# Routing of tokens to experts in four groups of tiles, with place masks made during attention and the weights gathered beside the rows

## The reference, cut to what matters

```python
x = x + attn(layernorm(x), ...)          # state space mixer, 64 heads
x = x + xattn(layernorm(x), ctx, ctx)    # 32 query heads, 8 key heads
x = x + ffn(layernorm(x), ...)

def ffn(x, router_logits, gating_einsum, linear, per_expert_scale, router_scale):
    router_input = x * rsqrt(mean(x * x) + 1e-6) * rsqrt(512) * router_scale
    logits = router_input @ router_logits                     # 8 experts
    probs = softmax(logits)
    choices = top_2(logits)
    weights = probs / sum(probs of the two chosen)
    # each token goes to its two experts: tokens are sorted by expert
    gate_out = rows @ w_gate[expert]                          # 512 -> 2 x 512
    activation = gelu(gate_out[0]) * gate_out[1]
    out = (activation @ linear[expert]) * per_expert_scale[expert]
    return sum over the two choices of weights * out
```

## Time and profile before

| | us |
|---|---|
| median of three runs | 1507.66 (1503.03 to 1511.12) |
| profiled execution | 1507.27 |
| its span | 1505.4 |
| mean granted TensorE clock | 0.937 of full |
| TensorE busy | 1345.9 |
| VectorE busy | 861.5 |
| ScalarE busy | 723.1 |
| GpSimd busy | 569.1 |

### The profile page before, as it was taken

How to read it: one execution, slowest core, us unless ns; L and a number is a source line. 1 busy time by engine, 2 the same in 40 slices (tenths; PEclk the granted TensorE clock), 3 DMA queues, 4 the chain that set the end, 5 groups by cost and what they waited for, 6 DMA issues and landing times.

```text
span 1505.4 us, 22777 instructions
## 1 busy us (share of the span) xinstructions
PE 1345.9 (89%) x7700; PEld 747.6 (50%) x7700; DVE 861.5 (57%) x1727; ACT 723.1 (48%) x1387; POOL 569.1 (38%) x852
## 2 busy tenths in 40 slices
PE   5699999999999999988788887854999999999997
PEld 4466566666666665653333333334444444444443
DVE  4887888879797978677888888335011111111111
ACT  2577666677676666672777766630111111111110
POOL 2355565645555547672233322123022222222221
PEclk9899999999999999997989889765999999999999
DMA  9000000000000000001000000012233444344322
GB/s 325 11 8 5 8 5 6 7 3 11 1 12 1 12 1 9 14 2 59 37 19 19 20 19 15 27 63 101 105 84 98 129 137 119 56 133 126 56 42 29
DMA packets 38017, 72.76 MB, mean 48 GB/s; under 512 B 16272, under 2 KB 20624, under 8 KB 36880
## 3 DMA queue, kind: packets, MB, share of 16 engines
q1 hardware_dynamic: 27968, 48.03, 9.0%
q0 software_dynamic: 8736, 20.45, 7.4%
q10 hardware_dynamic: 1200, 2.82, 0.5%
HBM read 148.75 MB, written 19.92 MB: 112 GB/s over the span
## 4 chain that ended last, share of the span: by engine, by line
PE 65%; DVE 18%; issue 5%; DMA 4%; POOL 4%; ACT 3%; SPq 0%; POOLq 0%; ACTq 0%; DVEq 0%
PE work_ps L502 11%; PE gate_ps L1377 9%; PE up_ps L1377 9%; PE down_ps L1365 9%; PE work_ps L574 6%; DVE conv L783 6%; PE work_ps L507 3%; PE work_ps L596 3%; PE work_ps L999 2%; DVE maxes L1148 2%; PE mturn_ps L507 2%; PE decay_ps L990 2%; DVE mix L699 2%; PE decay_ps L584 2%; DMA x_sb<-x_dram 1%
## 5 line engine op out<-in xcount | busy, mean ns | idle before, releaser
L502 PE MATMUL work_ps<-xnT,w_in 128*128 128x256 f32 (+1 forms) x1216 | 302.3, 394 | 1.6 <-DVE xdt L823 0.9
L699 POOL TENSOR_TENSOR mix<-decay,cbm 128x512 f32<-128x512 f32 x128 | 182.5, 1428 | 213.0 <-ACT decay L694 177.2
L502 PEld LDWEIGHTS work_ps<-xnT,w_in 128*128 128x128 f32 (+1 forms) x1216 | 220.8, 190 | 64.6 <-issue 33.3
L690 ACT ACTIVATE decay<-decay_ps 128x512 f32<-128x512 f32 x256 | 154.2, 603 | 110.2 <-PE decay_ps L584 108.8
L1148 DVE TENSOR_REDUCE maxes<-work_ps 128x2 f32<-128x512 f32 x256 | 166.7, 684 | 46.5 <-PE work_ps L975 45.5
L1507 POOL DMA_INDIRECT out_dram<-y_out,ids x39 | 61.8, 1586 | 337.4 <-DVE y_out L1476 270.4
L783 DVE SCALAR_TENSOR_TENSOR conv<-raw,conv_w,conv 128x256 f32<-128x256 f32 x240 | 179.7, 753 | 6.9 <-ACT conv L650 1.1
L1062 ACT ACTIVATE prob<-decay_ps 128x512 f32<-128x512 f32 x256 | 143.2, 607 | 81.3 <-PE decay_ps L990 80.1
L1483 DVE TENSOR_TENSOR act<-gelu,up_ps 128x512 f32<-128x512 f32 x39 | 26.8, 688 | 269.7 <-PE up_ps L1377 269.7
L694 ACT ACTIVATE decay<-decay 128x512 f32<-128x512 f32 x256 | 164.0, 641 | 4.7 <-PE work_ps L502 3.0
L1377 PE MATMUL gate_ps<-w_e,xgT 128*128 x312 | 143.1, 602 | 2.2 <-ACT xgT L1396 1.7
(11 more groups left out here) (253 smaller groups left out, 1893.6 us busy)
## 6 DMA issues: line engine op xcount, KB each, us to landing
w_e<-c_experts_dram SPq DMA_DIRECT2D x39, 3072.0 KB
normed_tokens<-r_xn SPq DMA_DIRECT2D x17, 256.0 KB, 2.2
out_dram<-x_sb SPq DMA_DIRECT2D x17, 256.0 KB, 3.0
x_sb<-x_dram SPq DMA_DIRECT2D x1, 3584.0 KB, 22.4
w_in<-c_w_inT_dram ACTq DMA_DIRECT2D x1, 2560.0 KB, 12.0
w_in<-c_w_inT_dram SPq DMA_DIRECT2D x1, 2048.0 KB, 8.5
w_out<-c_w_outT_dram SPq DMA_DIRECT2D x1, 2048.0 KB, 13.5
RT<-cum_scratch SPq DMA_DIRECT2D x32, 48.0 KB
```

Of the source, the lines that this page charges most:

```text
L502: m = e.matmul(ps[0:width, at:at + L], w_in[:, k, col:col + width], xnT[b % 2][:, k, :], start=(k == 0), stop=(k == KD - 1))
L690: e.activation(decay[s % 5][:, :], decay_ps[s % 3][:, :], ACT.Relu, scale=-1.0).then_inc(piece_done[stage], 1)
L699: return e.tensor_tensor(four(mix[s % 5]), four(decay[s % 5]), cb, ALU.mult)
```

## The change

The routing has four groups: tiles 0 to 7, 8 to 11, 12 to 13 and 14 to 15. The counting is done for each group by its own two matmuls ("c_count", TensorE, in one of the five shared banks), and "c_slots" (VectorE) adds the counts to those of the tiles before and gives the place of each token. So the place masks can be made by group: all 32 are made on GpSimd ("place"), 16 in batch 5 of the attention, 8 in batch 7, the rest behind it. The masks hold token numbers (less 2048) instead of ones and are f16; the second operand of the place matmuls is a plain mask of tiles, f16 with 39 columns. Unfilled slots get a number of their own.

For the last two tiles, VectorE adds the attention output of tile 14 and GpSimd that of tile 15 ("attend_v", "attend"). Their logits are made from centred rows ("last_center": the mean is taken off, no scale), and the scale of both norms is worked out beside it on VectorE ("last_newton") and applied to the logits. The router pieces of batch 6 stand four slots later (`late`).

The weights of the tokens are written as 8 more columns of normed_tokens ("c_weight_out"), whose rows grow from 512 to 520 numbers, and are gathered with the rows; in each expert tile VectorE picks the tile's column by two small operations (`row_weight`). The owners are worked out behind the token numbers. The copies of x_sb to the output are issued after each batch ("out_in"). Three memsets, a copy and an addition move into "r_init". Cut to its core:

```diff
-ROUTED = [(3, 0, 8), (6, 8, 14), (7, 14, 16)]
+ROUTED = [(3, 0, 8), (5, 8, 12), (6, 12, 14), (7, 14, 16)]
+ROUND = 1.5 * 2.0 ** 23 * P
...
+        if b == NB - 1:
+            continue
+        late = 4 if b == NB - 2 else 0
         put(f + 12, ("r_stats", b), ("r_newton", b))
         for t in range(TPB):
-            put(f + 16 + 2 * t, ("r_xn", b, t), ("r_store", b, t))
-            put(f + 17 + 2 * t, ("r_turn", b, t))
-            put(f + 18 + 2 * t, ("r_copy", b, t))
-            put(f + 19 + 2 * t, ("r_logit", b, t))
-            put(f + 20 + 2 * t, ("r_keep", b, t))
-    for g, (last, _, _) in enumerate(ROUTED):
-        f = n * (last + 1)
-        put(f + 20, ("c_scale", g), ("c_newton", g))
-        put(f + 26, ("c_logit", g), ("c_exp", g))
-        put(f + 28, ("c_rank", g))
-        put(f + 30, ("c_weight", g))
+            put(f + 16 + late + 2 * t, ("r_xn", b, t), ("r_store", b, t))
+            put(f + 20 + late, ("out_in", b, t))
+            put(f + 17 + late + 2 * t, ("r_turn", b, t))
+            put(f + 18 + late + 2 * t, ("r_copy", b, t))
+            put(f + 19 + late + 2 * t, ("r_logit", b, t))
+            put(f + 20 + late + 2 * t, ("r_keep", b, t))
...
+    for g, at in enumerate((4 * n + 20, 7 * n, 7 * n + 27)):
+        put(at, ("c_scale", g), ("c_newton", g))
+        put(at + 3, ("c_rank", g), ("c_count", g))
+        put(at + 5, ("c_logit", g), ("c_exp", g))
+        put(at + 6, ("c_slots", g))
+        if g < 2:
+            put(at + 9, ("c_weight", g), ("c_weight_out", g))
+    for t in range(12):
+        for c in range(2):
+            put(n * 5 + 4 * t if t < 8 else n * 7 + 8 + 4 * (t - 8) + 2 * c, ("place", c, t))
+    f = n * NB + 9
+    put(f, ("attend_v", NB - 1))
+    for t in range(TPB):
+        put(f, ("last_stats", t), ("last_center", t))
+    put(f, ("last_newton",), ("c_weight", 2), ("c_weight_out", 2), *[("place", c, t) for t in (12, 13) for c in range(2)])
+    for stage in ("r_turn", "r_copy", "r_logit"):
+        put(f, *[(stage, NB - 1, t) for t in range(TPB)])
+    for t in range(TPB):
+        put(f, ("r_xn", NB - 1, t), ("r_store", NB - 1, t), ("out_in", NB - 1, t), ("r_keep", NB - 1, t))
+    put(f, ("c_rank", 3), ("c_count", 3), ("c_logit", 3), ("c_exp", 3), ("c_slots", 3), *[("place", c, t) for t in (14, 15) for c in range(2)])
+    put(f, ("c_base",), ("c_spread", 0), ("c_weight", 3), ("c_weight_out", 3), ("c_spread", 1))
...
-    tokens = nc.dram_tensor("normed_tokens", [(NT + 1) * P, DIM], F32).ap()
+    tokens = nc.dram_tensor("normed_tokens", [(NT + 1) * P, DIM + NE], F32).ap()
...
+            elif stage == "c_count":
+                g, = key
+                _, first, end = ROUTED[g]
+                both = sel[2][:, first:end, :].rearrange("p t e -> p (t e)")
+                width = (end - first) * NE
+                e.wait_ge(*done("r_init"))
+                e.wait_ge(*done("c_rank", g))
+                e.matmul(work(*piece)[:, 0:width], m_ones[:, :], both, start=True, stop=True)
+                e.matmul(work(*piece)[:, NT * NE:NT * NE + width], earlier[:, :], both, start=True, stop=True).then_inc(piece_done[stage], 1)
...
+            elif stage == "last_center":
+                t, = key
+                e.wait_ge(*done("last_stats", t))
...
+                e.activation(a_xn[t][:, :], x_sb[:, (NB - 1) * TPB + t, :], ACT.Identity, bias=neg_mean[:, t:t + 1]).then_inc(piece_done[stage], 1)
...
+            elif stage == "attend_v":
+                b, = key
+                e.wait_ge(*done("pv_out", b, 3))
+                e.tensor_tensor(x_sb[:, b * TPB, :], x_sb[:, b * TPB, :], o_tok[b % 2][:, 0, :], ALU.add).then_inc(piece_done[stage], 1)
...
+            elif stage == "last_stats":
+                t, = key
+                tile = (NB - 1) * TPB + t
+                e.wait_ge(*done("attend" if t else "attend_v", NB - 1))
+                own.settle(e.bn_stats(r_bn[:, t, :], x_sb[:, tile, :]))
+                own.settle(e.bn_aggr(r_mv[:, tile, :], r_bn[:, t, :]))
+                e.tensor_scalar(neg_mean[:, t:t + 1], r_mv[:, tile, 0:1], -1.0, None, ALU.mult).then_inc(piece_done[stage], 1)
+            elif stage == "last_newton":
+                ts = slice((NB - 1) * TPB, NT)
+                e.tensor_scalar(last_rows[:, 0, 0, :], r_mv[:, ts, 1], LN_EPS, None, ALU.add)
+                own.settle(e.tensor_scalar(last_rows[:, 0, 1, :], r_mv[:, ts, 1], 1.0 + ROUTER_EPS, LN_EPS * ROUTER_EPS, ALU.mult, ALU.add))
+                rows = [last_rows[:, i, :, :].rearrange("p a t -> p (a t)") for i in range(3)]
+                own.settle(root_guess(e, own, *rows))
+                root_newton(e, own, *rows).then_inc(piece_done[stage], 1)
...
-                own.settle(e.tensor_tensor(weight[:, ts, :], weight[:, ts, :], e_scale[:, :].rearrange("p (o e) -> p o e", o=1).to_broadcast([P, n, NE]), ALU.mult))
...
-                m.then_inc(piece_done[stage], 1)
+                e.tensor_tensor(weight[:, ts, :], weight[:, ts, :], e_scale[:, :].rearrange("p (o e) -> p o e", o=1).to_broadcast([P, n, NE]), ALU.mult).then_inc(piece_done[stage], 1)
+            elif stage == "c_slots":
+                g, = key
+                _, first, end = ROUTED[g]
+                ts, n = slice(first, end), end - first
+                width, ps = n * NE, work("c_count", g)
+                e.wait_ge(*done("c_count", g))
+                for t in range(first, end):
+                    m = e.tensor_tensor(upto[:, t + 1, :], upto[:, t, :], ps[:, (t - first) * NE:(t - first + 1) * NE], ALU.add)
+                    own.settle(m)
+                own.settle(e.tensor_tensor(total[:, ts, :], upto[:, ts, :], ps[:, NT * NE:NT * NE + width].rearrange("p (t e) -> p t e", e=NE), ALU.add))
+                each = total[:, ts, :].rearrange("p (o t) e -> p o t e", o=1).to_broadcast([P, 2, n, NE])
+                own.settle(e.tensor_tensor(picked[:, :, 0:n, :], chosen[:, 0:2, ts, :], each, ALU.mult))
+                own.settle(e.reduce_sum(slot_of[:, :, ts], picked[:, :, 0:n, :], AX.X))
+                own.settle(e.tensor_scalar(rounded[:, :, ts], slot_of[:, :, ts], 0.5 - P // 2, ROUND, ALU.add, ALU.add))
+                e.scalar_tensor_tensor(place_of[:, :, ts], rounded[:, :, ts], -ROUND, slot_of[:, :, ts], ALU.add, ALU.subtract).then_inc(piece_done[stage], 1)
+            elif stage == "c_base":
+                own.settle(e.tensor_scalar(counts[:, 3, :], upto[:, NT, :], P // 2 - 0.5, ROUND, ALU.add, ALU.add))
+                own.settle(e.tensor_scalar(counts[:, 0, :], counts[:, 3, :], -ROUND, float(P), ALU.add, ALU.max))
+                own.settle(e.tensor_tensor_scan(counts[:, 1, :], f_ones[:, :], counts[:, 0, :], 0.0, ALU.mult, ALU.add))
+                own.settle(e.tensor_tensor(counts[:, 2, :], counts[:, 1, :], counts[:, 0, :], ALU.subtract))
+                bases = counts[:, 2, :].rearrange("p (a b e) -> p a b e", a=1, b=1).to_broadcast([P, 2, NT, NE])
+                own.settle(e.tensor_tensor(picked[:, :, :, :], chosen[:, 0:2, :, :], bases, ALU.mult))
+                own.settle(e.reduce_sum(tile_of[:, :, :], picked[:, :, :, :], AX.X))
+                own.settle(e.scalar_tensor_tensor(tile_of[:, :, :], rounded[:, :, :], -ROUND, tile_of[:, :, :], ALU.add, ALU.add))
+            elif stage == "c_spread":
+                c, = key
+                tiles = tile_id[:, :].rearrange("p (o i) -> p o i", o=1).to_broadcast([P, NT, MT])
+                e.tensor_tensor(own_tile[c][:, :, :], tiles, wide(tile_of[:, c, :]), ALU.is_equal).then_inc(piece_done[stage], 1)
...
+        def place_rows(e, c, t):
+            return e.tensor_scalar(places[c][t][:, :], row_id[:, :], place_of[:, c, t:t + 1], token_off[:, t:t + 1], ALU.is_equal, ALU.mult)
...
+            elif stage == "c_weight_out":
+                g, = key
+                _, first, end = ROUTED[g]
+                e.wait_ge(*done("c_weight", g))
+                e.dma_start(tokens[first * P:end * P, DIM:DIM + NE].rearrange("(t p) e -> p t e", p=P), weight[:, first:end, :]).then_inc(store_weights, 16)
+                if end == NT:
+                    e.dma_start(tokens[NT * P:(NT + 1) * P, DIM:DIM + NE], weight[:, NT - 1, :]).then_inc(store_weights, 16)
...
             for n, (c, t) in enumerate(PLACED):
                 if t == 0:
-                    e.wait_ge(spread, c + 1)
-                if t % 3 == 2:
-                    e.wait_ge(places_g, by_gpsimd.index(n) + 1)
-                else:
-                    e.wait_ge(places_v, by_vector.index(n) + 1)
-                e.matmul(mturn_ps[0][:, 0:2 * MT], places[n % 12][:, :], own_value[c][:, t, :, :], start=(n == 0), stop=(n == 2 * NT - 1)).then_inc(places_used, 1)
-            e.wait_ge(owners_known, 1)
-            e.wait_ge(rows_known, 1)
+                    e.wait_ge(*done("c_spread", c))
+                e.wait_ge(*done("place", c, t))
```

(11 more changed lines are left out.)

216 lines of the change are left out of this document (100 added, 116 removed).

## The result

The changed kernel takes 1485.93 us (median of 4 runs, 1481.74 to 1493.01) against 1509.39 of the kernel before beside it: a ratio of 0.9844, 95% interval 0.9809 to 0.9879. A second measurement of the same two kernels gave 0.9796 (0.9756 to 0.9837). The profiled execution took 1481.74, with a span of 1479.9. Forecast were 1478 and a range of 1468 to 1490; the forecast's own bounds were 1473 to 1484, and the median lies 2 above them.

The account below looks back on a forecast made before the run. TensorE, busy 89% of the span, was taken as the bound, with a serial chain of 49.6 us ahead of the expert tiles. 1507.27 - 28.5 (tail) - 0.5 (attention) = 1478.3, predicted 1478 us, range 1468 to 1490.

Parts of the forecast that it names:

- Tail: From the last attention output to the first gather: the shorter serial chain was to gain 28.5 us.
- The place matmuls: End of the tail: 32 f16 matmuls with 39 columns at 0.14 us each, the second 16 ending at 1018.4.
- The weights' store: Before the first gather: the store's 384 small rows land at 1026.8 and hold the gather, 1486 us; chance 0.05.
- The term of the last batch: Batch 7: batch 6's router stage four slots later removes TensorE's 2.9 us wait for normed rows; taken as -3 us.
- The clock's rival: Last batch: without the 2.9 us wait TensorE's clock may stay up, 6 us gained, 1472 us; chance 0.17.
- Group 0 and batches 1 to 6: Attention from the first score to the last maxima: moved routing work and place masks were to cost +2.5 us.
- the 3.8 allowed: Attention, group 0: TensorE waits up to 3.8 us at a counting matmul that stands behind the ranking.
- net +1.5 for VectorE's work: Attention: group 0's moved ranking, the counting wait and VectorE's slot operations, between -2.8 and +4, taken as +1.5 us.
- The masks' +1: Batch 5: sixteen place masks on GpSimd, a pair ahead of batch 4's root, cost 0 to 10 us, taken as +1.
- Expert tiles: After the first gather: two small VectorE operations more per tile were to cost nothing.
- attention pays: Attention: TensorE loses the full 3.8 us at group 0's count and the 2.9 wait stays, +9.4 us, 1488; chance 0.12.
- the 0.3 that the prediction put on the sum: Start of the tail: if the two residual adds exclude each other, 0.3 us longer with VectorE first.

Follow-up runs that it names:

- e3 kernels: Three kernels from e1_g1later_late0 with counts, weights and the masks of tiles 8 to 11 moved, two with further edits: 1484.83, 1482.52 and 1477.64 us.
- e1_g1later_late0: Changed kernel with tiles 8 to 11 routed later in the last batch and batch 6's router pieces at their old slots: 1480.83 us, ratio 0.9803.
- e3_split_add_late2: e1_g1later_late0 with counts, weights and masks moved, batch 6's residual add split between VectorE and GpSimd, its router pieces two slots later: 1477.64 us, ratio 0.9785.
- e1_again: The changed kernel measured once more, unedited: 1482.07 us, ratio 0.9796 to the kernel before.
- e2_wide_rows_only: The kernel before with only the rows of normed_tokens widened to 520 numbers, stored and gathered whole: 1511.18 us, ratio 1.0012.
- e1_g1later: Changed kernel with tiles 8 to 11 routed at slots 7n + 13 and on instead of 7n, their place masks later too: 1484.16 us, ratio 0.9817.

## Why the prediction was right, and where it was not

**Tail: the mechanism and nearly the size.** Forecast -28.5, measured -30.3. Last output to last logit: 8.7 forecast, 8.2 measured. From the last logit to the second tile mask: 9.0 forecast, 1012.69 to 1021.69 = 9.0 measured; counting dependent VectorE operations at 0.21 from start to start holds. The place matmuls were taken as 2.7 behind the second mask and took 0.8: 0.71 / 16 = 0.044 each, where I took 0.14. It lies outside the prediction's bounds of -1 to +2.6 for this term. The two bounds per matmul were the load of 128 columns (0.101) and a pass of the f32 form (0.217), and the truth lies below both; the loads overlap (0.60 for 16). This is the term that was mis-sized for the good, by 1.9. The masks on GpSimd took 0.80 at the median instead of 0.64 (a second operand from a column, f16 out), and were hidden, as said.

**The weights' store** holds the gather as that rival said, but for 0.6 us instead of 7.6: the second of the two stores landed 1.54 behind its issue, and all 384 rows of 32 bytes 1.96 behind the first, less than the 2.6 of the earlier trace rows. The rule on transfers under 512 bytes in the Trainium skill ("DMA: Bandwidth & Descriptors", "Specifications"), which spoke for this rival, shows no price here: stores of whole rows into the same tensor, 256 KB each, landed in 2.1 at the median. With the weights ahead of both masks (the e3 kernels) GpSimd starts 0.3 behind the ids, but these come 0.4 to 0.6 later, since the first 16 place matmuls lose their cover. Against the version that these kernels start from (19.2, e1_g1later_late0) nothing is gained.

**The term of the last batch is the one that failed.** "That removes TensorE's wait of 2.9 for the normed rows ... I take -3" came out as +3.8. Two things were wrong. The wait did not go: the rows were late too, for VectorE had the slots of tiles 8 to 11 ahead of batch 6's last output, a neighbour that the sum put at 0 because VectorE is idle two thirds of the time there; TensorE waited 2.73. And waits were not the price: TensorE's idle time in the batch fell by 0.6 and its busy time rose by 4.4, because the clock did not come back to 2.4 GHz before the last output. With the clock back the same batch takes 38.7 to 40.2, with waits for the rows of up to 5.1; with the clock down it takes 43.7 to 47.2 (40.9 without the masks). The sum had no term for when the clock comes back. The clock's rival ("the clock holds", -6) looked at the right quantity, but had the sign wrong and took the long wait for a condition of the fall, which e3_split_add_late2 speaks against. What brings the clock back stays open.

**Group 0 and batches 1 to 6.** +2.5 was forecast, +1.2 measured, and the stretch varies by up to 11 between profiles, so that agreement shows nothing. The waits tell more. In batch 4 the wait of 2.81 became 3.45 (2.59 in e1_again), within the 3.8 allowed. But a second one came behind it, for the negated maxima, where the kernel before had 1.29:

```profile
886.92 0.37 PE L1012 MATMUL work_ps<-ident,nmax 128*32 128x128 f16 x2 [2.86 <-DVE nmax L1210]
```

It is 2.3 to 2.9 in every profile with the counting by group. The sum had it only as a part of its net +1.5 for VectorE's work. What it is worth can't be read from the length of the batch, which moves with the clock: 41.4 us before, 44.1 after, but 43.7 in e2_wide_rows_only, which has the old order. The masks' +1 came as 1.1 of waiting. VectorE's slot operations for group 0 are 13 and not 14.

**Expert tiles.** Nothing was forecast and nothing came; the -1.7 behind the gather is mostly the first gate product, 5.33 instead of 6.24, as the clock rises sooner.

**Sum.** 1507.27 - 30.3 + 3.8 + 1.5 + 1.2 - 1.7 = 1481.8, the profiled execution. The error of 3.5 against 1478.3 is +6.8 from the last batch, +1.5 ahead of the first score, -1.3 from there to the last maxima, -1.8 in the tail and -1.7 behind the gather. That the errors of the tail, of batches 1 to 6 and of the expert tiles have the other sign is luck, and so is a part of the closeness. Attention came out at +5.0 where -0.5 was forecast, halfway to the +9.4 of the rival "attention pays", whose condition that the wait of 2.9 stays came true. The median of the four runs lies 4 higher still, that of e1_again at this 1482.

**A better version.** The kernel of e3_split_add_late2 has 58.5 us from the last maxima to the gather against 63.2, and the lowest median of all runs, 1477.64. Its interval overlaps that of e1_again, so it is faster than the kernel before by 2.2% and not shown to beat the changed one.

## What to carry to other kernels

A serial tail of small dependent operations can be forecast by counting them at their start-to-start time, and two cheap moves shorten it: apply a scale after the product instead of before it, and do for earlier tiles what needs no later one. Where TensorE runs in two clock levels, moving work by a few slots can go with several us of either sign that no wait shows; measure such a stretch between two events of the trace and split it into busy and idle time of the bounding engine, since the total time of a run hides it. Moving work away from one wait can make another: look for the engine that passes the work on in order. Before putting a price of zero on work in an idle engine, look at what stands right behind it on that engine.

## What the runs showed of the hardware

The clock fell to 1.2 GHz in the last batch of every version: at 972 in e3_split_add_late2, with no TensorE wait above 1.1, and at 979 in the changed kernel, 1.3 us into a wait of 2.7. It was back for good some 10 to 17 us later in some, in others not before the end of attention. In the four profiles whose pieces in this batch are those of the changed kernel it took 43.7 to 43.8 us.

VectorE's small operations with two inputs in SBUF stand still while GpSimd adds two tiles. The changed kernel, in batch 7:

```profile
970.78 2.50 POOL L1392 TENSOR_TENSOR x_sb<-x_sb,o_tok 128x512 f32<-128x512 f32 x2 [3.65 <-DVE o_tok L1230]
970.83 0.18 DVE L1311 TENSOR_REDUCE mean_sq<-weight 128x4 f32<-128x32 f32 x1
971.05 0.18 DVE L1312 RECIPROCAL mean_sq<-mean_sq 128x4 f32<-128x4 f32 x1
971.26 0.83 DVE L1313 TENSOR_TENSOR weight<-weight,mean_sq 128x32 f32<-128x32 f32 x1
972.13 1.20 DVE L1314 TENSOR_TENSOR weight<-weight,e_scale 128x32 f32<-128x32 f32 x1
```

The operations with one input take 0.18 here. Those with two take 0.83 and 1.20 instead of the 0.19 of e1_g1later, and end at 972.09 and 973.33, where GpSimd's first and second add end (972.03 and 973.28). The other way round, GpSimd's add of the last tile took 1.77 instead of 1.25, having started 0.05 behind VectorE's of 0.69. This is the exclusion that "SBUF — State Buffer" of the Trainium skill states in "Who interferes with whom", and here it is seen at both ends: with VectorE first, GpSimd's add was 0.5 longer, and the 0.3 that the prediction put on the sum by that rule did not show, because tile 15 was not the one waited for. One input is no safeguard, though: the step of the variance in batch 5 (0.17 us alone, one input) took 1.25 beside GpSimd's work on xnT and ended with it.
